# A row of maxima by VectorE's 32x32 transposition in an attention kernel

## What is computed

```
Q = xn @ proj_q[h];  K = xn @ proj_k;  V = xn @ proj_v        # 8 heads, one K and one V for all
weights = softmax(Q @ K.T)                                   # 1024 x 1024 per batch and head
Y = sum over h of (weights @ V) @ proj_o[h].T
F = sum over 8 experts of (xn @ w1[e]) @ w2[e]                # no activation between them
out = x + Y + F
```

## Time and profile before

| | |
|---|---|
| profiled execution / its span | 1669.67 us / 1667.9 us |
| TensorE matmul busy | 1634.7 us, 98% |
| TensorE weight load busy | 1214.1 us, 73% |
| VectorE busy | 1239.3 us, 74% |
| ScalarE busy | 1304.2 us, 78% |
| GpSimd busy | 1379.9 us, 83% |
| granted clock, 100 to 1600 us | 1.00 |
| chain that ended last, by engine | GpSimd 56%, issue 24%, TensorE 18% |

### The profile page before, as it was taken

The page is one execution under the profiler, slowest core; times in us unless marked ns, Lnnn a source line. Parts: engine busy times, 40 slices in busy tenths (PEclk is TensorE's granted clock), DMA queues, the critical chain, the costliest instruction groups (busy, mean ns, idle before and its releaser), DMA issues.

```text
span 1667.9 us, 46510 instructions
## 1 busy us (share of the span) xinstructions
PE 1634.7 (98%) x18820; PEld 1214.1 (73%) x18820; DVE 1239.3 (74%) x2655; ACT 1304.2 (78%) x1350; POOL 1379.9 (83%) x1008
## 2 busy tenths in 40 slices
PE   7999999999999999999999999999999999999998
PEld 6777777777777777777777777777777777777775
DVE  5777777777777777777777777777777777777775
ACT  4777877787787788778778777877878787787785
POOL 2788888888888888888888888888888888878876
PEclk9999999999999999999999999999999999999999
DMA  8000000000000000000000000000000000000000
GB/s 230 2 2 2 1 2 14 2 2 2 2 15 2 2 2 3 13 2 2 2 8 8 2 2 1 8 8 2 2 2 8 8 2 2 2 14 2 2 1 14
DMA packets 16769, 16.73 MB, mean 10 GB/s; under 512 B 432, under 2 KB 12976, under 8 KB 16560
## 3 DMA queue, kind: packets, MB, share of 16 engines
q1 hardware_dynamic: 15520, 13.24, 2.7%
q10 hardware_dynamic: 1040, 0.52, 0.1%
HBM read 9.57 MB, written 4.19 MB: 8 GB/s over the span
## 4 chain that ended last, share of the span: by engine, by line
POOL 56%; issue 24%; PE 18%; ACT 1%; DVE 0%; POOLq 0%; DMA 0%; SPq 0%; DVEq 0%; ACTq 0%
POOL pr_lo L306 40%; POOL xacc L318 9%; POOL xn L300 3%; PE s_ps L548 2%; PE s_ps L550 2%; PE s_ps L535 2%; PE t_ps L586 2%; PE t_ps L589 2%; PE t_ps L588 2%; POOL rstd L345 2%; POOL xacc L324 1%; POOL xn_lo L290 1%; PE s_ps L432 1%; PE s_ps L434 1%; PE s_ps L433 1%
## 5 line engine op out<-in xcount | busy, mean ns | idle before, releaser
L306 POOL TENSOR_TENSOR pr_lo<-pr,pr_hi 128x1024 f16<-128x1024 f32 x511 | 1086.4, 2134 | 264.3 <-ACT pr_hi L396 264.3
L389 ACT ACTIVATE pr<-s_ps,boost,scale 128x1024 f32<-128x1024 f32 x512 | 616.8, 1205 | 211.1 <-PE s_ps L550 210.3
L778 DVE TENSOR_REDUCE key_max<-s_ps 128x128 f16<-128x1024 f32 x512 | 624.0, 1219 | 0.0
L396 ACT ACTIVATE pr_hi<-pr 128x1024 f16<-128x1024 f32 x512 | 525.4, 1051 | 8.1
L548 PE MATMUL s_ps<-g_lo,xT 128*128 128x128 f16 x4096 | 512.4, 219 | 1.1 <-DVE g_lo L791 1.1
L550 PE MATMUL s_ps<-g_hi,xT 128*128 128x128 f16 x4096 | 512.3, 219 | 0.0
L548 PEld LDWEIGHTS s_ps<-g_lo,xT 128*128 128x128 f16 x4096 | 400.7, 98 | 31.6 <-DVE g_lo L791 1.6
L550 PEld LDWEIGHTS s_ps<-g_hi,xT 128*128 128x128 f16 x4096 | 400.8, 98 | 29.7
L586 PE MATMUL t_ps<-pr_hi,xn_hi 128*128 128x512 f16 x1024 | 388.7, 380 | 16.3 <-POOL pr_lo L306 14.4
L588 PE MATMUL t_ps<-pr_lo,xn_hi 128*128 128x512 f16 x1024 | 388.1, 379 | 0.0
L589 PE MATMUL t_ps<-pr_hi,xn_lo 128*128 128x512 f16 x1024 | 388.1, 379 | 0.0
(11 more groups left out here) (123 smaller groups left out, 1602.7 us busy)
## 6 DMA issues: line engine op xcount, KB each, us to landing
out_dram<-xacc SPq DMA_DIRECT2D x16, 256.0 KB, 2.3
w_sb<-in_L_ffn_w_dram SPq DMA_DIRECT2D x1, 2048.0 KB, 10.2
pr<-in_L_attn_proj_q_dram ACTq DMA_DIRECT2D x1, 512.0 KB, 4.7
xacc<-in_L_attn_x_dram SPq DMA_DIRECT2D x2, 256.0 KB, 5.1
pr<-in_L_attn_proj_o_dram SPq DMA_DIRECT2D x1, 512.0 KB, 6.5
xacc<-in_L_attn_x_dram SPq DMA_DIRECT2D x1, 384.0 KB, 11.0
xacc<-in_L_attn_x_dram SPq DMA_DIRECT2D x1, 128.0 KB, 6.3
wkv<-in_L_attn_proj_k_dram SPq DMA_DIRECT2D x1, 64.0 KB, 2.9
```

What stands on the lines that cost most here:

```text
L306: pool.tensor_tensor(pr_lo[:, u % RING, :], pr32[:, u % PR, :], pr_hi[:, u % RING, :], ALU.subtract)\
L389: act.activation(pr32[:, u % PR, :], both_banks(u), ACT.Exp, bias=boost[:, 0:1], scale=scale[:, 0:1])\
L396: act.activation(pr_hi[:, u % RING, :], pr32[:, u % PR, :], ACT.Copy).then_inc(p_hi_ready, 1)
L778: dve.tensor_reduce(key_max[:, u % 2, :], both_banks(u).rearrange("p (t q) -> p q t", q=P), AX_X, ALU.max).then_inc(keys_max, 1)
```

## The change

- TensorE no longer makes a row of the maxima: `max_to_row` and its matmul go. `turn_keys_max(n)` moves ahead of `low_passes(n - 1)`, and waits for max_found(n - 1) in place of the bias; where at is 3 it waits for t_lo as well. The second chunk stands behind the low passes in one piece in every period.
- VectorE's `place_bias` moves from the head of the next period to right behind `find_max`. It transposes minus_max, now 128x32 (the maxima in column 0, zeros beside them), in 32x32 blocks into max_rows, whose partitions 0, 32, 64 and 96 then hold 32 maxima each, and copies these four pieces into partition 0 of g_lo. The bias semaphore counts four for each unit.
- The tile's statistics get a second slot (`ln_slot`), and the power, the scaling and the low half on GpSimd go to periods 8p + 8, 8p + 9 and 8p + 13 for the tile of pair p, ScalarE's high half to 8p + 11.

```diff
@@ shapes and semaphores
-        minus_max = sb("minus_max", [P, 2, P], F16)
+        minus_max = sb("minus_max", [P, 2, QUAD], F16)
+        max_rows = sb("max_rows", [P, 2, QUAD], F16)
...
@@ gpsimd
-                if n % 8 == 2 and (tile := ln_tile(n // 8)) is not None:
-                    pool.wait_ge(ln_var, tile - AHEAD + len(FIRST_TILES) + 1)
-                    pool.tensor_tensor(rstd[:, AHEAD:AHEAD + 1], var_eps[:, AHEAD:AHEAD + 1],
-                                       minus_half[:, 0:1], ALU.pow).then_inc(ln_rstd, 1)
-                if n % 8 == 3 and (tile := ln_tile(n // 8)) is not None:
-                    normalise_next(tile)
-                if n % 8 == 7 and (tile := ln_tile(n // 8)) is not None:
-                    xn_low(tile, 0, 1)
+                if (tile := ln_tile(n // 8 - 1)) is not None:
+                    if n % 8 == 0:
+                        slot = ln_slot(tile)
+                        pool.wait_ge(ln_var, tile - AHEAD + len(FIRST_TILES) + 1)
+                        pool.tensor_tensor(rstd[:, slot:slot + 1], var_eps[:, slot:slot + 1], minus_half[:, 0:1], ALU.pow)\
+                            .then_inc(ln_rstd, 1)
+                    if n % 8 == 1:
+                        normalise_next(tile)
+                    if n % 8 == 5:
+                        xn_low(tile, 0, 1)
@@ scalar
-                if n % 8 == 6 and (tile := ln_tile(n // 8)) is not None:
+                if n % 8 == 3 and (tile := ln_tile(n // 8 - 1)) is not None:
                     split_high(tile, 0, 1)
@@ tensor
-                pe.wait_ge(bias_ready, u + 1)
+                pe.wait_ge(bias_ready, (P // QUAD) * (u + 1))
...
                 pe.wait_ge(keys_max, u + 1)
                 if u >= 1:
-                    pe.wait_ge(bias_ready, u)
+                    pe.wait_ge(max_found, u)
+                if u % 4 == 3 and summing(u) >= 1:
+                    pe.wait_ge(t_lo_ready, summing(u))
...
-                        pe.wait_ge(bias_ready, min(4 * k + 6, UNITS))
+                        pe.wait_ge(max_found, min(4 * k + 6, UNITS))
...
                 if n < UNITS:
                     high_pass(n, 0)
-                if 1 <= n <= UNITS and at != 3:
-                    max_to_row(n - 1)
-                if n < UNITS:
                     high_pass(n, 1)
-                if 1 <= n <= UNITS and at == 3:
-                    max_to_row(n - 1)
                 chunk(n, 0)
                 small_products(n)
+                if n < UNITS:
+                    turn_keys_max(n)
                 if 1 <= n <= UNITS:
                     low_passes(n - 1)
-                if at == 2:
-                    chunk(n, 1, rest=False)
-                if n < UNITS:
-                    turn_keys_max(n)
-                chunk(n, 1, first=at != 2)
+                chunk(n, 1)
@@ vector
             def place_bias(u):
                 k, j = divmod(u, 4)
-                dve.wait_ge(rowed, u + 1)
+                dve.wait_ge(max_found, u + 1)
+                dve.transpose(max_rows[:, u % 2, :], minus_max[:, u % 2, :]).then_inc(max_turned, 1)
+                dve.wait_ge(max_turned, u + 1)
                 if j == 0:
                     dve.wait_ge(g_lo_ready, k + 1)
-                dve.tensor_copy(g_lo[0:1, k % 2, j * P:(j + 1) * P], maxima_row(u)[0:1, :]).then_inc(bias_ready, 1)
+                for a in range(P // QUAD):
+                    at = j * P + a * QUAD
+                    dve.tensor_copy(g_lo[0:1, k % 2, at:at + QUAD], max_rows[a * QUAD:a * QUAD + 1, u % 2, :])\
+                       .then_inc(bias_ready, 1)
...
-                if 1 <= n <= UNITS:
-                    place_bias(n - 1)
                 if n < UNITS:
                     max_of_keys(n)
                 between_maxima(n)
                 if n < UNITS:
                     find_max(n)
+                    place_bias(n)
                 before_bias(n)
```

More of the change, by code:

```diff
@@ L40, in attention_ffn @@
     BANK = 512
+    QUAD = 32
     SB = 6
@@ L66, in attention_ffn @@
         xn32 = sb("xn32", [P, AHEAD, D], F32)
[L67 to L70, removed]
+        stats = sb("stats", [P, AHEAD + 2, 6], F32)
+        mean_var = sb("mean_var", [P, AHEAD + 2, 2], F32)
+        var_eps = sb("var_eps", [P, AHEAD + 2], F32)
+        rstd = sb("rstd", [P, AHEAD + 2], F32)
         minus_half = sb("minus_half", [P, AHEAD], F32)
@@ L129, in attention_ffn @@
         g_ps, g_hi_ready, g_lo_ready = sem("g_ps"), sem("g_hi_ready"), sem("g_lo_ready")
-        high_done, keys_max, turned, max_found, rowed, bias_ready = (
-            sem(n) for n in ("high_done", "keys_max", "turned", "max_found", "rowed", "bias_ready"))
+        high_done, keys_max, turned, max_found, max_turned, bias_ready = (
+            sem(n) for n in ("high_done", "keys_max", "turned", "max_found", "max_turned", "bias_ready"))
         scores_ready, exp_done, p_hi_ready, p_lo_ready = (
@@ L192, in maxima_turned @@
             return turn_bank(u)[:, 0:P // 2].bitcast(F16)
-        def maxima_row(u):
-            return turn_bank(u + 1)[:, 2 * P:3 * P]
         def ffn_tile(n):
@@ L214, in turn_tile, with ln_slot @@
             return pair + NT if at == 0 and pair >= 1 and pair + NT < TILES else None
+        def ln_slot(tile):
+            return AHEAD + tile % 2
         def ln_tile(pair):
@@ L299, in normalise_next @@
                 pool.wait_ge(xn_ready, tile)
-                pool.tensor_scalar(xn32[:, 0, 1:D], xacc[:, tile, 1:D], mean_var[:, AHEAD, 0:1],
-                                   rstd[:, AHEAD:AHEAD + 1], ALU.subtract, ALU.mult).then_inc(ln_xn32, 1)
+                slot = ln_slot(tile)
+                pool.tensor_scalar(xn32[:, 0, 1:D], xacc[:, tile, 1:D], mean_var[:, slot, 0:1],
+                                   rstd[:, slot:slot + 1], ALU.subtract, ALU.mult).then_inc(ln_xn32, 1)
             def p_low(u):
@@ L561, in turn_keys_max @@
                 pe.transpose(maxima_turned(u), key_max[:, u % 2, :], ident16[:, :]).then_inc(turned, 1)
[L563 to L569, removed]
             def weigh(k, t, first, rest):
@@ L861, in before_bias @@
                         dve.wait_ge(x_in[4], 16)
-                    dve.bn_stats(stats[:, AHEAD, :], xacc[:, tile, :]).then_inc(ln_stats, 1)
+                    dve.bn_stats(stats[:, ln_slot(tile), :], xacc[:, tile, :]).then_inc(ln_stats, 1)
                 if at == 1 and (tile := ln_tile(pair)) is not None:
                     dve.wait_ge(ln_stats, tile + 1)
-                    dve.wait_ge(ln_xn32, tile)
-                    tile_mean(AHEAD)
+                    dve.wait_ge(ln_xn32, tile - 1)
+                    tile_mean(ln_slot(tile))
                 if at == 3 and (tile := ln_tile(pair)) is not None:
                     dve.wait_ge(ln_mean, tile + 1)
-                    dve.tensor_scalar_add(var_eps[:, AHEAD:AHEAD + 1], mean_var[:, AHEAD, 1:2], EPS).then_inc(ln_var, 1)
+                    slot = ln_slot(tile)
+                    dve.tensor_scalar_add(var_eps[:, slot:slot + 1], mean_var[:, slot, 1:2], EPS).then_inc(ln_var, 1)
                 if n == 0:
```

## The result

The changed kernel takes 2561.06 us (median of four, 2548.47 to 2564.81) against 1669.44 us of the kernel before beside it: ratio 1.533, 95% interval 1.531 to 1.535, +892 us. The forecast was 1970 with a range to 2450; the direction was right, the size was not.

A forecast was written before the change was run, and what follows sets the result against it. TensorE, nearly full, was taken to bound the kernel at 12.68 us per block. Closed chain 14.04, VectorE's string 0.2 and copies' waits 0.8 gave 15.04, +300 us over 127 blocks: 1970 us, range 1840 to 2450.

The forecast's parts named there:

- The chain closed by the new order: TensorE waits each period for key_max before turn, low passes and second chunk: 3.51 us per period, 14.04 per block, +173 us.
- The row's 512 slots of 0.06: TensorE's removed maximum-row matmuls: 29 us of slots, worth nothing once TensorE waits in every period.
- VectorE's string: Maximum, transposition and four copies on VectorE end too late in the period with the projection: +0.2 us per block, 25 us.
- The tile's earlier scaling: Power and normalisation leave GpSimd's pr_lo burst; the saving falls within TensorE's 23 us of pr_lo waits, gone anyway.
- What the copies meet: VectorE's copies wait for GpSimd's running pr_lo, then all four of a group pass: 0.8 us per block.
- The rival that says this: GpSimd gets an instruction in between VectorE's copies: 19.5 us per block, about 2530 us; one let in per group, 2270; chance 0.28.
- The row read as "never waits": VectorE's L870, one SBUF input, one column, never waits for GpSimd; ground for a no-waiting rival, 1843 to 1932 us, chance 0.30.
- The lower clock: Sign to look for: granted clock below 1.00 in the middle stretches, a cost that no case holds.

The follow-up runs named there:

- run 6: Changed kernel with the turn behind the low passes, copies as reductions, and the tile's work where it was before: 1694.86 us, ratio 1.015.
- run 4: Changed kernel with the turn of key_max behind the low passes and the four copies written as reductions: 1728.26 us, ratio 1.035.
- run 2: Changed kernel with its four copies written as reductions over an axis of length 1, all else as it is: 1914.10 us, ratio 1.147.
- run 1: Kernel before with only the order changed: turn of key_max ahead of the low passes, second chunk in one piece behind them: 1920.02 us, ratio 1.150.
- dose: Kernel before plus four VectorE copies per period that nobody waits for: 2357.33 us from four quadrants, 1967.59 all from partition 0.
- run 8: Kernel before with the tile's power and scaling in period 8p + 4, high half in 8p + 7, low half in 8p + 8: 1646.08 us, ratio 0.986.
- runs of 7: Kernel before plus four unused VectorE operations per period: copies from four quadrants 2357.33 us, copies from partition 0 1967.59, reductions 1679.74.

## Why the prediction was wrong

**The path of the loss**, taken one cause after another: 1669 to 1695 for the row on VectorE (+26, run 6), to 1728 for the tile's earlier scaling (+33, run 4), to 1914 for the order (+186, run 2), to 2561 for the copies' waits (+647). The prices depend on the order in which they are added: the turn's place costs 251 alone (run 1), 186 with reductions and 265 with copies; the copies' waits 568 with the late turn, 688 as a dose.

- **The chain closed by the new order**: right in mechanism and near in size. I worked out 3.51 per period; measured is 3.54 where nothing else is late (run 2). The estimate of +173 stands against 186 between runs 4 and 2, and against 251 in run 1, where the row's matmul and copy stand in the chain as well. (The row's 512 slots of 0.06 are 31 us, not 29; the sum does not use them.)
- **VectorE's string**: the transposition was taken at 0.21 and is 0.212 (below), the copies at 0.15 each and are 0.166 where nothing is in the way, 0.75 per group. The period with the projection is late by 0.23 to 0.25, forecast 0.2.

```profile
L785 DVE STREAM_TRANSPOSE max_rows<-minus_max 128x32 f16<-128x32 f16 x512 | 108.5, 212 | 17.8
```

- **The tile's earlier scaling** was put at a small saving. That was wrong: I looked at what it takes out of GpSimd's burst (0.45 per pair, and run 8 shows this worth 23 us) and not at its new deadline, the transposition three periods on, with GpSimd two to three periods behind.
- **What the copies meet** is the step that failed. The mechanism was named and is shown. The size was not: I took 0.8 us per block, assuming that all four copies of a group pass once GpSimd's instruction has ended, because in the one case of the trace VectorE went first. It did so for one instruction. In its place the runs show GpSimd getting in between two copies, and (2561 - 1914)/127 = 5.1 us per block. The rival that says this gave 19.5 per block and 2530 in all; measured are 19.43 and 2561. Its mechanism is right, but that its sum is so near is in part luck. It forecast periods of 7.3, 5.2, 3.5 and 3.5 in each block; the reductions follow each other at 4.45, 4.47, 3.53, 4.51, 6.88, 5.04, 3.64 and 6.33 us through a pair, 16.96 for one block and 21.89 for the next. And the measured time holds the lower clock and the tile's 33 us, which its sum lacks. It had a chance of 0.28, and the range was cut at 2450 with 0.13 left above; one row against it was too little for that.
- **The row read as "never waits"**, L870, was no guide. All its 54 started within an operation of GpSimd on two tensors and took 0.145 us at most, but the copies, which also have one SBUF input, wait. L870 has one column and another operation; no run varies what sets them apart.
- **The lower clock** was named as a cost that no number held. 2271 of TensorE's 18308 slots are at the 1.2 GHz level, by the distances from start to start; at 0.052 more for 128 columns and 0.21 for 512 these are 181 us at most. How much of that lies on the path and not ahead of a wait is not settled: no run separates it from the stalls that it comes with. It is inside the 647.

The rule of the Trainium skill, "SBUF — State Buffer", section Who interferes with whom, on which a sentence of the prediction stood, is now shown for this shape: a copy with a single SBUF input, 1x32 of 16 bits, waits for GpSimd's whole instruction, and a reduction never does. The rule exempts no operation of GpSimd that reads SBUF, but copies passed within the scaling L304 in 54 of 54 cases; here the measurement decides. "VectorE: DVE Perf Modes", on two Vector instructions with no wait between them, has an instruction held whose input starts in another quadrant. The dose in one quadrant (1968 us against 2357 from four) agrees with it: in one quadrant two copies share a turn, from four each needs its own.

## What to carry to other kernels

An engine's idle share does not say that small work is free there: ask behind whose 2 us instruction the new one may have to wait, and price that per instruction, not per group. Where GpSimd is busy with elementwise work on two tensors, move small things between partitions of SBUF by an operation that was seen not to wait; a reduction over an axis of length 1 cost 0.17 us and never waited. And before work is moved later for relief, look who consumes it and how far the engine that makes it runs behind.

## What the runs showed of the hardware

- A 128x32 transposition of 16 bits on VectorE takes 0.212 us, a copy of 1x32 0.166 and a reduction to 1x32 0.174 in the median, all SBUF to SBUF.
- A copy of 0.166 us becomes up to 2.08 us behind a GpSimd instruction of 2.13. All 571 long copies stood behind an operation on two tensors; none was held by the scaling of one tensor, 0.83 us long, or by the power of one column. The 512 transpositions (0.211 to 0.215 us) and the reductions were never held.
- Between two copies from different quadrants GpSimd gets one instruction in, and from one partition two copies pass at a time (runs of 7).
- In the main loop of the changed kernel, each of the 69 stalls of TensorE's matmuls over 3 us (4.8 at most) was followed by a stretch at 1.2 GHz. In runs 1 and 2, whose stalls there are 0.7 and 1.0 us at most, the granted clock stayed at 1.00. Such a stall is not the only thing seen before it: the dose from one partition has none over 2.5 us there and falls to 1.2 GHz in 20 stretches from 1627 us on.
